# A cross-attention block on one NeuronCore: SBUF tiles at other addresses, softmax exponentials divided on GpSimd before they are turned, no turned inverses

## The chip, the cores and the metric

The kernel runs on one core of a Trainium2 chip. The metric is the device time of one execution in microseconds (us). Engines are named as the profile names them: PE (TensorE, with its weight loads as PEld), DVE (VectorE), ACT (ScalarE), POOL (GpSimd) and SP (SyncE, which here only issues DMAs). All arithmetic is fp32, with matrix products made of three fp32r products of high and low halves.

## The reference

128 sequences of 128 rows and 256 features go through one block: layer norm, self-attention of 16 heads of 16 features, a gated-in memory product, a second layer norm, and a feed-forward of 1024 hidden features. Cut to what matters:

```python
tgt1 = _layer_norm(tgt, g1, be1)
q = (x @ Wq.T + bq).reshape(b, s, H, HD)      # k and v alike
score = jnp.einsum('bshd,bthd->bhst', q, k) / math.sqrt(HD)
score = score + (1.0 - mask[:, None, :, :]) * -1000000000.0
p = jax.nn.softmax(score, axis=-1)
o = jnp.einsum('bhst,bthd->bshd', p, v).reshape(b, s, d)
tgt = tgt + (o @ Wo.T + bo)
tgt = tgt + (memory @ Wg.T + bg)
tgt1 = _layer_norm(tgt, g2, be2)
ff = jax.nn.relu(tgt1 @ W1.T + b1) @ W2.T + b2
return tgt + ff
```

The softmax needs, for each row of each head, the sum of 128 exponentials; the place where it is divided by that sum is free, since the division commutes with the product by v.

## The kernel before, in words

Two sequences make a group (GB = 2), so there are 64 groups. The program is written out as iterations i = -2 ... 65, and in iteration i five stages run side by side on different groups: `norm` (layer norm statistics of group i+2), `front` (turn, q, k and v of group i+1), `attn_` (scores and softmax of group i), `out_` (values, output projection, second layer norm of group i-1) and `ffn` (feed-forward of group i-2). Each iteration is cut into 13 ticks. Every engine has its own loop over the ticks, and tables such as `EXP_TICKS` and `TURN_TICKS` say at which tick it issues which piece. Nothing else sets the order: within an engine instructions run strictly in the order written, and across engines semaphores hold them.

A group has 8 chunks of 4 heads. A chunk k goes this way: PE writes its scores into one of two PSUM banks (`scores_of`), DVE adds the mask bias, takes the row minimum and writes to a ring of `scores` slots in SBUF ("mask k" below, L604), ACT takes exponentials in place with their row sums (`exponentials`, "exp k", L367, four instructions), PE turns the four 128x128 blocks into one of two `turn_ps` banks (`turn_chunk`, L850), and ACT copies them to `probs` (`copy_turned`, L377). The values product (`values_of`, L876) comes once all eight are copied.

The division before: DVE inverts the sums of four chunks at once (`invert_sums`, L547), POOL spreads them to 16 columns a head (`spread_inverses`, `inv_rows`, L704), PE turns those (`turn_inverses`, L860, four transposes), ACT copies the result to `inv` (L385), and DVE multiplies the finished values by `inv` while it takes them out of PSUM (`attn`, L624), then makes `attnT_hi` (L628) and `attnT_lo` (L567) from `attn`.

Other pieces that the prediction speaks of: `k_hi` on ACT (L436) and `k_lo`, `q_lo` on DVE (L651, L643), after which SP copies q and k into `q_stack` and `k_stack` by DMA for the next iteration's scores; `hT_hi` (DVE L634) and `hT_lo` (POOL L713), the halves of the hidden layer, four of each an iteration (numbered 0 to 3), that the down product waits for; `memT_hi` and `memT_lo` on POOL (L732, L713); `x_res` on POOL (L745), which `resid` on DVE (L577) waits for; then the second layer norm: `stats` (DVE L524), `var` and `rstd` (POOL L695, L697), `xhat2` (DVE L539, shown as xhat), and its turn on PE (L804), then the last quarter of the down product ("down3").

Of the kernel before, what the change touches and what calls it, by code (L numbers as in the profile page):

```python
# [45 lines left out]
INVERT_TICKS = (5, 9)  # L46
TURN_TICKS = (3, 4, 5, 7, 9, 10, 12)
# [21 lines left out]
def xattn_block(nc, x, memory, mask, wqT, wkT, wvT, woT, wgT, w1T, w2T,  # L69
# [13 lines left out]
    RING = 5  # L83
# [10 lines left out]
    with ExitStack() as ctx:  # L94
# [12 lines left out]
        vector_cols, at = {}, 0
        vec = sb("vec", [P, sum(n for _, n in VECTORS)])
        for name, n in VECTORS:
            vector_cols[name] = vec[:, at:at + n]  # L110
            at += n
        g1c, be1c, g2c, be2c, _, _, b1c = (vector_cols[name] for name, _ in VECTORS[:-1])
        qk_bias = sb("qk_bias", [P, 2 * KT])
        bqc, bkc = qk_bias[:, 0:KT], qk_bias[:, KT:2 * KT]
# [16 lines left out]
        stats1, mv1 = sb("stats1", [P, GB, 6]), sb("mv1", [P, GB, 2])  # L131
        var1, var2 = sb("var1", [P, GB]), sb("var2", [P, GB])
# [12 lines left out]
        row_min = sb("row_min", [P, CHUNKS, CH])  # L145
        row_sum, sum_inv = sb("row_sum", [P, CHUNKS, CH]), sb("sum_inv", [P, GB, KT, CPB, 2])

        inv_rows = sb("inv_rows", [P, GB, KT, P])
        be1w = inv_rows[:, 0]
        carrier = sb("carrier", [P, CHUNKS])  # L150
# [9 lines left out]
        stats2, mv2 = sb("stats2", [P, GB, 6]), sb("mv2", [P, GB, 2])  # L160
        rstd1, rstd2 = sb("rstd1", [P, GB]), sb("rstd2", [P, GB])
        one = sb("one", [P, H])
        eps, minus_half = sb("eps", [P, GB]), sb("minus_half", [P, GB])
        xhat2 = sb("xhat2", [P, GB, D])
        zT = [sb("zT_hi", [P, KT, ROWS], F32R), sb("zT_lo", [P, KT, ROWS], F32R)]
# [4 lines left out]
        y = sb("y", [P, GB, D])  # L170

# [33 lines left out]
        inv_spread = sem("inv_spread")  # L205
        inv_turned, inv_copied, attn_ready = sem("inv_turned"), sem("inv_copied"), sem("attn_ready")
# [51 lines left out]
        def loaded(name):  # L258
# [5 lines left out]
            if name in "qko":  # L264
                return {"q": attn, "k": inv, "o": resid}[name][:].rearrange("p k r -> p (k r)")
# [80 lines left out]
        def _(act):  # L346
# [33 lines left out]
            def copy_inverses(g):  # L380

                act.wait_ge(inv_turned, g + 1)
                if later(g):
                    act.wait_ge(attn_ready, g)
                act.activation(inv[:].rearrange("p k r -> p (k r)"), turn_ps[0][:, :], ACT.Copy  # L385
                               ).then_inc(inv_copied, 1)

            def iteration(i, norm, front, attn_, out_, ffn):
                for t in range(TICKS):
                    if out_ and t == 0:  # L390
                        copy_turned(i - 1, CHUNKS - 1)
                    if out_ and t == 1:
                        copy_inverses(i - 1)
# [8 lines left out]
                    if attn_ and t == 7:  # L402
                        copy_turned(i, TURN_TICKS.index(t))
# [9 lines left out]
                    if attn_ and t in TURN_TICKS and t != 7:  # L413
                        copy_turned(i, TURN_TICKS.index(t))
# [43 lines left out]
        def _(dve):  # L458
# [545 lines left out]
```

## Time and profile before

| | |
|---|---|
| median of 3 runs | 1834.77 us (1831.8 to 1836.27) |
| the profiled execution's own time | 1833.82 us |
| its span in the trace | 1832.2 us |
| PE busy, weight loads busy | 97%, 95% |
| ACT, DVE, POOL busy | 80%, 74%, 47% |
| SP's DMA queue (q1), share of 16 engines | 60.6% |
| granted TensorE clock, mean of the span | 0.989 |

Busy shares are of the span. The first 95 us and the last 35 us are ramps in which fewer than five stages run; between them each engine repeats one pattern of a little over 27 us, once for each group.

### The profile page before, as it was taken

To read this page: it belongs to the slowest core of one execution; us is meant where nothing else is said; L and a number is where in the kernel's file an instruction comes from. 1 tells how busy PE (TensorE), PEld (TensorE's weight loads), DVE (VectorE), ACT (ScalarE), POOL (GpSimd) and SP (SyncE) were. 2 spreads that over 40 slices of the span, in tenths; PEclk is the share of its full clock that TensorE was granted. 3 is DMA by queue.
4 is the path that set the end of the run, shared out by engine and by line. 5 is a ranking of instruction groups with operands and counts; after the bars stand their busy time and mean duration, and the time that the engine had idled before them with its cause. 6 is when DMAs were issued, how large, how long until landed. Compare 5 with 4: busy or idle time off the path is not lost.

```text
span 1832.2 us, 53739 instructions
## 1 busy us (share of the span) xinstructions
PE 1779.9 (97%) x17972; PEld 1746.4 (95%) x17972; DVE 1357.0 (74%) x6810; ACT 1464.7 (80%) x5577; POOL 867.6 (47%) x907
## 2 busy tenths in 40 slices
PE   5699999999999999999999999999999999999997
PEld 4699999999999999999999999999999999999997
DVE  5677777777777777777777777777777777777772
ACT  2788888887887888888887887888888887887882
POOL 2244544544544544544444444444454454454454
PEclk7799999999999999999999999999999999999999
DMA  6656656656656656656656656756756756756740
GB/s 157 84 87 112 98 98 110 98 98 110 99 98 109 99 98 110 100 98 109 100 98 108 104 96 106 107 93 107 110 92 105 109 93 105 112 91 103 110 71 18
DMA packets 148931, 183.66 MB, mean 100 GB/s; under 512 B 14768, under 2 KB 99120, under 8 KB 148656
## 3 DMA queue, kind: packets, MB, share of 16 engines
q1 hardware_dynamic: 148656, 180.23, 60.6%
q8 instruction: 144, 2.36, 0.6%
q14 instruction: 131, 1.07, 0.2%
HBM read 62.73 MB, written 16.78 MB: 43 GB/s over the span
## 4 chain that ended last, share of the span: by engine, by line
PE 95%; ACT 2%; issue 1%; DVE 0%; ACTq 0%
PE ffn_ps L787 13%; PE ffn_ps L789 13%; PE ffn_ps L788 13%; PE turn_ps L850 12%; PE work_ps L787 9%; PE work_ps L789 8%; PE work_ps L788 8%; PE score_ps L836 7%; PE value_ps L876 7%; PE work_ps L804 3%; PE turn_ps L860 2%; ACT scores L367 1%; ACT hid L410 0%; ACT probs L377 0%; DVE y L589 0%
## 5 line engine op out<-in xcount | busy, mean ns | idle before, releaser
L367 ACT ACTIVATE scores<-scores,row_min 128x128 f32<-128x128 f32 x2048 | 795.6, 400 | 8.9 <-DVE row_min L604 3.6
L713 POOL TENSOR_TENSOR hT_lo<-hid,hT_hi 128x512 fp32r<-128x512 f32 x256 | 355.4, 1388 | 587.5 <-DVE hT_hi L634 587.5
L377 ACT ACTIVATE probs<-turn_ps 128x512 f32<-128x512 f32 x512 | 303.0, 593 | 241.9 <-PE turn_ps L850 241.9
L604 DVE CUSTOM_DVE_ANT_0 scores<-score_ps,mask_bias 128x128 f32<-128x128 f32 x2048 | 470.8, 285 | 2.0 <-issue 2.0
L367 ACT ACTIVATION_READ_ACCUMULATOR scores<-scores,row_min 128x1 f32 x2048 | 407.0, 199 | 0.0
L850 PE MATMUL turn_ps<-ident,scores 128*128 128x128 f32 x2048 | 308.9, 274 | 4.5 <-ACT probs L377 4.5
L787 PE MATMUL ffn_ps<-zT_hi,w_lo 128*128 128x256 f32 x1024 | 304.2, 297 | 5.0 <-ACT hid L410 4.2
L787 PE MATMUL ffn_ps<-w_hi,hT_lo 128*128 128x256 f32 x1024 | 302.3, 295 | 2.4 <-ACT hid L410 2.4
L789 PE MATMUL ffn_ps<-zT_hi,w_hi 128*128 128x256 f32 x1024 | 289.5, 283 | 0.0
L788 PE MATMUL ffn_ps<-zT_lo,w_hi 128*128 128x256 f32 x1024 | 288.0, 281 | 0.0
L789 PE MATMUL ffn_ps<-w_hi,hT_hi 128*128 128x256 f32 x1024 | 286.6, 280 | 0.0
L788 PE MATMUL ffn_ps<-w_lo,hT_hi 128*128 128x256 f32 x1024 | 286.3, 280 | 0.0
L850 PEld LDWEIGHTS turn_ps<-ident,scores 128*128 128x128 f32 x2048 | 237.4, 141 | 5.7 <-ACT scores L367 5.5
L410 ACT ACTIVATE hid<-ffn_ps,vec 128x256 f32<-128x256 f32 x512 | 211.9, 467 | 22.4 <-PE ffn_ps L789 18.3
L836 PE MATMUL score_ps<-k_stack,q_stack 128*128 128x256 f32 x1024 | 200.3, 288 | 21.8 <-issue 12.9
L634 DVE CAST hT_hi<-hid 128x512 fp32r<-128x512 f32 x256 | 107.9, 421 | 146.1 <-ACT hid L410 146.1
L787 PEld LDWEIGHTS ffn_ps<-zT_hi,w_lo 128*128 128x128 f32 x1024 | 193.4, 189 | 6.7 <-ACT hid L410 5.2
L787 PEld LDWEIGHTS ffn_ps<-w_hi,hT_lo 128*128 128x128 f32 x1024 | 193.0, 188 | 3.0 <-ACT hid L410 3.0
L788 PEld LDWEIGHTS ffn_ps<-zT_lo,w_hi 128*128 128x128 f32 x1024 | 193.4, 189 | 0.0
L788 PEld LDWEIGHTS ffn_ps<-w_lo,hT_hi 128*128 128x128 f32 x1024 | 193.1, 189 | 0.0
L789 PEld LDWEIGHTS ffn_ps<-w_hi,hT_hi 128*128 128x128 f32 x1024 | 192.5, 188 | 0.0
L789 PEld LDWEIGHTS ffn_ps<-zT_hi,w_hi 128*128 128x128 f32 x1024 | 192.1, 188 | 0.0
(113 smaller groups left out, 4262.6 us busy)
## 6 DMA issues: line engine op xcount, KB each, us to landing
q_stack<-q_hi SPq DMA_DIRECT2D x128, 256.0 KB, 7.0
k_stack<-k_hi SPq DMA_DIRECT2D x256, 128.0 KB, 6.6
x_in<-x_dram SPq DMA_DIRECT2D x64, 256.0 KB, 3.4
mem_in<-memory_dram SPq DMA_DIRECT2D x64, 256.0 KB, 7.3
x_res<-x_dram SPq DMA_DIRECT2D x64, 256.0 KB, 7.5
q_stack<-q_lo SPq DMA_DIRECT2D x64, 256.0 KB, 4.2
k_stack<-k_lo SPq DMA_DIRECT2D x128, 128.0 KB, 6.6
out_dram<-y SPq DMA_DIRECT2D x64, 256.0 KB, 2.3
```

The lines of the kernel that those rows point to most:

```text
L367: last = act.activation(exps, exps, ACT.Exp, bias=row_min[:, k, h:h + 1], scale=-1.0, accum_out=row_sum[:, k, h:h + 1])
L377: act.activation(probs[:, k, :], turn_ps[k % 2][:, :], ACT.Copy).then_inc(probs_copied, 1)
L410: last = act.activation(hid[:, n % 2, j, :], ffn_ps[:, j * ROWS:(j + 1) * ROWS], ACT.Relu, bias=b1c[:, 2 * n + j:2 * n + j + 1])
L604: last = dve.tensor_tensor_reduce(out=scores[:, slot(i, t), h, :], in0=score_ps[t % 2][:, h * S:(h + 1) * S], in1=mask_bias[:, b, :], scal ...
L634: dve.tensor_copy(hT[0][:, 2 * n:2 * n + 2, :], hid[:, n % 2]).then_inc(hid_hi, 1)
L713: pool.tensor_tensor(halves[1], src, halves[0], ALU.subtract).then_inc(done, 1)
L787: pe.matmul(dst, lhs[1], rhs[0], start=start and j == 0, stop=False, **more)
L788: pe.matmul(dst, lhs[0], rhs[1], start=False, stop=False, **more)
L789: last = pe.matmul(dst, lhs[0], rhs[0], start=False, stop=stop and j == n - 1, **more)
L836: last = pe.matmul(score_ps[n % 2][:, k * 2 * S:(k + 1) * 2 * S], q_stack[i % 2][:, c, k, seq(b)], k_stack[i % 2][:, c, :, GB * k + b, :], ...
L850: last = pe.transpose(turn_ps[k % 2][:, h * S:(h + 1) * S], scores[:, slot(g, k), h, :], ident[:])
L876: last = pe.matmul(value_tiles[32 * c:32 * (c + 1), k, seq(b)], v_pad[g % 2][:, b, head_of(c, h), :], probs[:, CPB * b + c, h * S:(h + 1) ...
```

## The change

Three things are changed.

The division moves. DVE now inverts each chunk's four sums by themselves, right after that chunk's exponentials (eight reciprocals of 128x4 an iteration instead of two of 128x16). POOL then multiplies the chunk's 128x512 exponentials by them, in place in the ring (`divide`, eight instructions of 128x512 an iteration). PE waits for that (`exps_divided`) before it turns a chunk. `inv_rows`, `turn_inverses`, the copy to `inv` and the multiplication into `attn` are gone; `attnT_hi` and `attnT_lo` are made straight from PSUM, each a tick later.

The turns are one tick later (`TURN_TICKS`), the last chunk's turn and its copy move from tick 0 to tick 1 of the next iteration, the values product from tick 1 to 2; the ring has 7 slots instead of 5.

The SBUF tensors are declared in another order, with the small ones together. Before, the large tiles start at addresses that are 32, 64, 96 or other multiples of 32 past a multiple of 512 bytes: the weights 256, xT, q, k, the stacks and the ring 416, attnT and memT 320, zT, hid and hT 96. After, every large tile starts at a multiple of 512.

```diff
-INVERT_TICKS = (5, 9)
-TURN_TICKS = (3, 4, 5, 7, 9, 10, 12)
+INVERT_TICKS = (1, 2, 3, 4, 6, 7, 8, 10)
+DIVIDE_TICKS = (1, 2, 3, 4, 6, 7, 8, 10)
+TURN_TICKS = (4, 5, 6, 8, 9, 11, 12)
...
-    RING = 5
+    RING = 7
...
             def iteration(i, norm, front, attn_, out_, ffn):
                 for t in range(TICKS):
-                    if out_ and t == 0:
+                    if out_ and t == 1:
                         copy_turned(i - 1, CHUNKS - 1)
-                    if out_ and t == 1:
-                        copy_inverses(i - 1)
...
-            def invert_sums(i, b):
-                dve.wait_ge(exps_ready, CHUNKS * i + CPB * (b + 1))
+            def invert_sums(i, k):
+                dve.wait_ge(exps_ready, CHUNKS * i + k + 1)
                 if later(i):
-                    dve.wait_ge(inv_spread, GB * (i - 1) + b + 1)
-                dve.reciprocal(sum_inv[:, b], row_sum[:, CPB * b:CPB * (b + 1), :]
-                               .rearrange("p c (k e) -> p k c e", k=KT)).then_inc(sums_inverted, 1)
+                    dve.wait_ge(exps_divided, CHUNKS * (i - 1) + k + 1)
+                dve.reciprocal(sum_inv[:, k, :], row_sum[:, k, :]).then_inc(sums_inverted, 1)
...
-                    if out_ and t == 2:
+                    if out_ and t == 3:
                         g = i - 1
                         dve.wait_ge(attended, g + 1)
-                        dve.wait_ge(inv_copied, g + 1)
-                        if later(g):
-                            dve.wait_ge(attnT_split, g)
-                        dve.tensor_tensor(attn[:], value_tiles, inv[:], ALU.mult).then_inc(attn_ready, 1)
-                        dve.wait_ge(attn_ready, g + 1)
                         if later(g):
                             dve.wait_ge(proj_ready, g)
-                        dve.tensor_copy(attnT[0][:], attn[:]).then_inc(attnT_hi, 1)
+                        dve.tensor_copy(attnT[0][:], value_tiles).then_inc(attnT_hi, 1)
...
-                    if out_ and t == 3:
-                        split_low(attn[:], attnT, attnT_hi, i, attnT_split)
+                    if out_ and t == 4:
+                        split_low(value_tiles, attnT, attnT_hi, i, attnT_split)
...
-            def spread_inverses(g, b):
...
+            def divide(i, k):
+
+                pool.wait_ge(sums_inverted, CHUNKS * i + k + 1)
+                exps = scores[:, slot(i, k), :, :]
+                pool.tensor_tensor(exps, exps, sum_inv[:, k, :].unsqueeze(2).broadcast_to([P, CH, S]), ALU.mult
+                                   ).then_inc(exps_divided, 1)
...
-                    if attn_ and t == 6:
-                        spread_inverses(i, 0)
-                    if attn_ and t == 10:
-                        spread_inverses(i, 1)
+                    if attn_ and t in DIVIDE_TICKS:
+                        divide(i, DIVIDE_TICKS.index(t))
...
-                pe.wait_ge(exps_ready, CHUNKS * g + k + 1)
-                if k == 0 and later(g):
-                    pe.wait_ge(inv_copied, g)
+                pe.wait_ge(exps_divided, CHUNKS * g + k + 1)
...
-                    if out_ and t == 0:
+                    if out_ and t == 1:
                         turn_chunk(i - 1, CHUNKS - 1)
-                        turn_inverses(i - 1)
...
-                    if out_ and t == 1:
+                    if out_ and t == 2:
                         values_of(i - 1)
```

What stands in POOL's row, in a middle iteration, from tick 3 on. Before, from hT_lo 1 and 2 to the second spread; sums_inverted comes from DVE, ln2_mean from DVE's statistics of resid:

```order
L713 TENSOR_TENSOR hT_lo<-hid,hT_hi 128x512 [waits s_hid_hi] x2
L704 TENSOR_TENSOR inv_rows<-sum_inv,one 128x256 [waits inv_turned,sums_inverted]
L745 TENSOR_TENSOR x_res<-x_res,row 128x512 [waits xres_loaded]
L695 TENSOR_TENSOR var<-mv,eps 128x2 [waits ln2_ready,ln2_mean]
L697 TENSOR_TENSOR rstd<-var,minus_half 128x2 [waits ln2_var]
L713 TENSOR_TENSOR hT_lo<-hid,hT_hi 128x512 [waits s_hid_hi]
L695 TENSOR_TENSOR var<-mv,eps 128x2 [waits ln1_ready,ln1_mean]
L697 TENSOR_TENSOR rstd<-var,minus_half 128x2 [waits ln1_var]
L704 TENSOR_TENSOR inv_rows<-sum_inv,one 128x256 [waits inv_turned,sums_inverted]
```

The same stretch in the changed kernel, from divisions 2 and 3 to division 7:

```order
L682 TENSOR_TENSOR scores<-scores,sum_inv 128x512 [waits sums_inverted] x2
L688 TENSOR_TENSOR hT_lo<-hid,hT_hi 128x512 [waits s_hid_hi]
L682 TENSOR_TENSOR scores<-scores,sum_inv 128x512 [waits sums_inverted]
L718 TENSOR_TENSOR x_res<-x_res,row 128x512 [waits xres_loaded]
L682 TENSOR_TENSOR scores<-scores,sum_inv 128x512 [waits sums_inverted]
L674 TENSOR_TENSOR var<-mv,eps 128x2 [waits ln2_ready,ln2_mean]
L676 TENSOR_TENSOR rstd<-var,minus_half 128x2 [waits ln2_var]
L688 TENSOR_TENSOR hT_lo<-hid,hT_hi 128x512 [waits s_hid_hi]
L682 TENSOR_TENSOR scores<-scores,sum_inv 128x512 [waits sums_inverted]
L674 TENSOR_TENSOR var<-mv,eps 128x2 [waits ln1_ready,ln1_mean]
L676 TENSOR_TENSOR rstd<-var,minus_half 128x2 [waits ln1_var]
L682 TENSOR_TENSOR scores<-scores,sum_inv 128x512 [waits sums_inverted]
```

Division 4 now stands ahead of x_res, division 5 between x_res and the second layer norm's root, division 6 behind hT_lo 3; each waits for a reciprocal of DVE.

What stands in DVE's row around attnT_lo, before: tick 3, behind the second hT_hi and ahead of q_lo.

```order
L634 CAST hT_hi<-hid 128x512 [waits s_hid_relu]
L567 TENSOR_TENSOR attnT_lo<-attn,attnT_hi 128x512 [waits s_attnT_hi]
L643 SCALAR_TENSOR_TENSOR q_lo<-work_ps,qk_bias,q_hi 128x256 [waits q_high]
L643 SCALAR_TENSOR_TENSOR q_lo<-work_ps,qk_bias,q_hi 128x256
L601 MEMSET carrier 128x1 [waits scores_ready,probs_turned]
```

And in the changed kernel, from the second half of q_lo to attnT_lo in tick 4 (the rows between are mask 4, and the reciprocal is number 3):

```order
L622 SCALAR_TENSOR_TENSOR q_lo<-work_ps,qk_bias,q_hi 128x256
L585 MEMSET carrier 128x1 [waits scores_ready,probs_turned]
L588 ISA scores,row_min<-score_ps,mask_bias 128x128
L588 ISA row_min 128x1
L588 ISA scores,row_min<-score_ps,mask_bias 128x128
L588 ISA row_min 128x1
L588 ISA scores,row_min<-score_ps,mask_bias 128x128
L588 ISA row_min 128x1
L588 ISA scores,row_min<-score_ps,mask_bias 128x128
L588 ISA row_min 128x1
L532 RECIPROCAL sum_inv<-row_sum 128x4 [waits exps_divided,exps_ready]
L551 TENSOR_TENSOR attnT_lo<-value_ps,attnT_hi 128x512 [waits s_attnT_hi]
```

attnT_lo now stands behind mask 4 and behind a reciprocal that waits for the exponentials of chunk 3.

## Rows read from the trace of the kernel before

**Rows 1.** Busy time in the steady stretch: PE, PEld, DVE, ACT, POOL; then clock, DMA
```profile
400.00:800.00 400.00, 398.35 (x4082) 392.28 (x4075) 304.55 (x1546) 333.24 (x1278) 195.72 (x203) 1.00 0.63 101
```
**Rows 2.** Timeline of PE in one iteration: start us, length us, instructions, xcount
```profile
889.68 0.71 PE L836 MATMUL score_ps<-k_stack,q_stack 128*128 128x256 f32 x4 [0.44 <-issue]
...
890.67 0.60 PE L860 MATMUL turn_ps<-ident,inv_rows 128*128 128x128 f32 x4
891.10 0.60 PE L804 MATMUL work_ps<-ident,xhat 128*128 128x128 f32 x4
...
900.48 0.60 PE L850 MATMUL turn_ps<-ident,scores 128*128 128x128 f32 x4
...
902.95 0.36 PE L787 MATMUL work_ps<-wo_hi,attnT_lo 128*128 128x256 f32 x1
...
916.98 0.71 PE L836 MATMUL score_ps<-k_stack,q_stack 128*128 128x256 f32 x4
```
**Rows 3.** Timeline of PEld: weight loads of two products, first and last of each
```profile
903.62 0.19 PEld L787 LDWEIGHTS work_ps<-wg_hi,memT_lo 128*128 128x128 f32 x1
...
904.30 0.31 PEld L836 LDWEIGHTS score_ps<-k_stack,q_stack 128*128 128x128 f32 x2
...
909.92 0.19 PEld L787 LDWEIGHTS ffn_ps<-w_hi,hT_lo 128*128 128x128 f32 x1
...
911.20 0.19 PEld L789 LDWEIGHTS ffn_ps<-w_hi,hT_hi 128*128 128x128 f32 x1
```
**Rows 4.** DMA issues of the page: count, size, median us from issue to landing
```profile
k_stack<-k_hi SPq DMA_DIRECT2D x256, 128.0 KB, 6.6
```
**Rows 5.** Timeline of ACT around exp 3
```profile
900.68 0.84 ACT L436 ACTIVATE k_hi<-work_ps,qk_bias 128x256 fp32r<-128x256 f32 x2 [0.19 <-PE work_ps L789]
901.40 0.40 ACT L367 ACTIVATE scores<-scores,row_min 128x128 f32<-128x128 f32 x1
...
902.95 0.58 ACT L377 ACTIVATE probs<-turn_ps 128x512 f32<-128x512 f32 x1
```
**Rows 6.** Timeline of DVE, from mask 5 on
```profile
902.94 0.29 DVE L604 CUSTOM_DVE_ANT_0 scores<-score_ps,mask_bias 128x128 f32<-128x128 f32 x1
...
906.00 0.28 DVE L604 CUSTOM_DVE_ANT_0 scores<-score_ps,mask_bias 128x128 f32<-128x128 f32 x1
...
908.57 0.69 DVE L577 TENSOR_TENSOR resid<-work_ps,x_res 128x512 f32<-128x512 f32 x1 [1.65 <-issue]
...
910.34 0.29 DVE L604 CUSTOM_DVE_ANT_0 scores<-score_ps,mask_bias 128x128 f32<-128x128 f32 x1
...
911.47 0.73 DVE L539 TENSOR_SCALAR xhat<-resid,mv,rstd 128x256 f32<-128x256 f32 x2 [0.20 <-POOL rstd L697]
912.12 0.42 DVE L634 CAST hT_hi<-hid 128x512 fp32r<-128x512 f32 x1
912.99 0.25 DVE L547 RECIPROCAL sum_inv<-row_sum 128x16 f32<-128x16 f32 x1 [0.45 <-ACT scores L367]
```
**Rows 7.** Timeline of POOL
```profile
896.44 1.05 POOL L732 TENSOR_TENSOR memT_hi<-mem_in,one 128x512 fp32r<-128x512 f32 x1
...
905.37 1.29 POOL L713 TENSOR_TENSOR hT_lo<-hid,hT_hi 128x512 fp32r<-128x512 f32 x1 [3.16 <-DVE hT_hi L634]
...
907.19 1.29 POOL L745 TENSOR_TENSOR x_res<-x_res,row 128x512 f32<-128x512 f32 x1
910.46 0.19 POOL L695 TENSOR_TENSOR var<-mv,eps 128x2 f32<-128x2 f32 x1 [1.98 <-DVE mv L531]
```
**Rows 8.** Timeline of DVE, attnT_hi
```profile
896.54 1.23 DVE L628 CAST attnT_hi<-attn 128x512 fp32r<-128x512 f32 x1
```
**Rows 9.** Busy times by stretch, columns as in rows 1
```profile
57.60:61.00 3.40, 1.63 (x13) 1.18 (x11) 0.51 (x6) 3.40 (x16) 0.00 (x0) 1.00 1.03 140
...
88.30:95.00 6.70, 3.21 (x15) 3.24 (x16) 3.05 (x13) 0.84 (x2) 1.00 (x1) 0.50 0.86 168
...
1797.00:1822.00 25.00, 19.23 (x149) 17.81 (x148) 7.88 (x16) 5.68 (x14) 13.29 (x12) 1.00 0.04 12
```

More of the change, by code:

```diff
@@ L102, in sem @@
             return ctx.enter_context(nc.semaphore(name))
+        row_min = sb("row_min", [P, CHUNKS, CH])
+        row_sum, sum_inv = sb("row_sum", [P, CHUNKS, CH]), sb("sum_inv", [P, CHUNKS, CH])
         ident = sb("ident", [P, P])
[L107 to L114, printed above, removed]
         row = sb("row", [P, 4, D])
@@ L144, in xattn_block @@
         scores = sb("scores", [P, RING, CH, S])
[L145 to L150, printed above, removed]
         probs = sb("probs", [P, CHUNKS, CH * S])
-        inv = sb("inv", [P, KT, ROWS])
-        attn = sb("attn", [P, KT, ROWS])
+        early = sb("early", [P, KT * D])
         attnT = [sb("attnT_hi", [P, KT, ROWS], F32R), sb("attnT_lo", [P, KT, ROWS], F32R)]
@@ L159, in xattn_block @@
         resid = sb("resid", [P, GB, D])
[L160 to L163, printed above, removed]
         xhat2 = sb("xhat2", [P, GB, D])
+        be1w = xhat2[:, 0, :].rearrange("p (k s) -> p k s", k=KT)
         zT = [sb("zT_hi", [P, KT, ROWS], F32R), sb("zT_lo", [P, KT, ROWS], F32R)]
@@ L170, in xattn_block @@
         y = sb("y", [P, GB, D])
+        vector_cols, at = {}, 0
+        vec = sb("vec", [P, sum(n for _, n in VECTORS)])
+        for name, n in VECTORS:
+            vector_cols[name] = vec[:, at:at + n]
+            at += n
+        g1c, be1c, g2c, be2c, _, _, b1c = (vector_cols[name] for name, _ in VECTORS[:-1])
+        qk_bias = sb("qk_bias", [P, 2 * KT])
+        bqc, bkc = qk_bias[:, 0:KT], qk_bias[:, KT:2 * KT]
+        stats1, mv1 = sb("stats1", [P, GB, 6]), sb("mv1", [P, GB, 2])
+        var1, var2 = sb("var1", [P, GB]), sb("var2", [P, GB])
+        carrier = sb("carrier", [P, CHUNKS])
+        stats2, mv2 = sb("stats2", [P, GB, 6]), sb("mv2", [P, GB, 2])
+        rstd1, rstd2 = sb("rstd1", [P, GB]), sb("rstd2", [P, GB])
+        one = sb("one", [P, H])
+        eps, minus_half = sb("eps", [P, GB]), sb("minus_half", [P, GB])
         score_ps = [bank("score_ps0"), bank("score_ps1")]
@@ L264, in loaded @@
             if name in "qko":
-                return {"q": attn, "k": inv, "o": resid}[name][:].rearrange("p k r -> p (k r)")
+                return early[:] if name == "k" else {"q": resid_b2, "o": resid}[name][:].rearrange("p b n -> p (b n)")
             at, n = {"v": (0, 1), "1": (1, 4)}[name]
@@ L852, in turn_chunk @@
                 last.then_inc(probs_turned, 1)
-            def turn_inverses(g):
-                pe.wait_ge(inv_spread, GB * (g + 1))
-                pe.wait_ge(probs_copied, CHUNKS * g + CHUNKS - 1)
-                for k in range(KT):
-                    for b in range(GB):
-                        last = pe.transpose(turn_ps[0][:, k * ROWS + b * S:k * ROWS + (b + 1) * S],
-                                            inv_rows[:, b, k, :], ident[:])
-                last.then_inc(inv_turned, 1)
             def values_of(g):
```

25 lines of the change are left out of this document (3 added, 22 removed).

## The prediction

> **What bounds the kernel now.** I read the busy shares by stretch first. Between the ramps PE is busy 398.4 of 400 us, ACT 333, DVE 305, POOL 196 [rows 1]: PE has no room, the others do. Then PE's timeline: an iteration is 27.30 us from score product to score product, with a wait of 0.44 us ahead of the first one [rows 2]. The trace names no releaser for that wait. The product also waits for k_stack, whose six copies SP issues one after the other behind k_lo and which land 6.6 us after their issue [rows 4], so I put it down to them: PE's work sets the period, and the k_stack copies come a few tenths late in some iterations. Last I read ACT, DVE and POOL around the places that the change touches, since a division put between exponential and turn makes POOL part of every chunk's path.
>
> **What PE is spared.** turn_inverses takes 891.10 - 890.67 = 0.43 us an iteration [rows 2], 64 times 27 us. The copy to inv (ACT) and the product attn (DVE) go too, but these engines wait for PE now, so they give nothing by themselves.
>
> **Addresses.** Six steps of the product of memT by wg take 904.30 - 903.62 = 0.68 us, 0.113 a step; eleven of hT by w2 take 1.28, 0.116 [rows 3]. The first pair lies at 320 and 256 past multiples of 512, the second at 96 and 256: where one operand starts at an odd multiple of 32 bytes the step is longer by 0.003 to 0.006. With all at 512 I take 0.113 for all. Some 150 of 172 such steps an iteration would gain 0.004: 0.6 us, 0.3 of it ahead of the k projection's end. Bounds: nothing, and 1.0 us if steps fall below 0.113. "SBUF — State Buffer", section "Door 1: The DMA port swizzle", of the Trainium skill says that reads cost by lines of 16 bytes; all operands start at multiples of 32 already, so by that rule the addresses change no step and the period below would be 30.7 instead of 30.4. Rows 3 speak mildly against the rule.
>
> **The division's own price.** POOL has no row of this form. memT_hi, 128x512 with one operand spread over the columns, takes 1.05 us; x_res, with two full operands, 1.29 [rows 7]. The division spreads one operand, so I take 1.05 and keep 1.29 as the upper bound. Eight of them are 8.4 us; POOL goes from 13.4 us an iteration (196 of 400 [rows 1]) less the two spreads to about 20.6 of 27. By busy time it fits. The order is what matters, since POOL and DVE run strictly in the order written.
>
> **One iteration, step by step, in us after its first score product** (step lengths are differences of starts in the rows):
> First, the k projection ends at 10.80 (900.48 - 889.68 [rows 2]) before; without the inverses and with chunk 0's turn now behind it, 0.43 each, and 0.3 for addresses, at 9.65. Up to here PE is the limit.
> Second, k_hi and exp 3 follow on ACT, 902.95 - 900.48 = 2.47 [rows 5], and the last sum 0.1 later: 12.2. DVE inverts (0.25 for 16 columns [rows 6], I take 0.2): 12.4. Now attnT_lo stands behind this reciprocal. Nearest row is resid, which reads PSUM at the same size: 0.69 [rows 6]. It is ready at 13.1. PE reaches the output projection after chunk 0's turn, an up product, a score product and chunk 1's turn, which took 902.95 - 900.48 = 2.47 before too [rows 2]: at 12.0. **Wait A: 1.1 us.**
> Third, DVE goes on with mask 5, statistics, hT_hi and k_lo, 906.00 - 902.94 = 3.06 [rows 6] less the reciprocal of 0.16 that is no longer there: 16.0. Mask 6 and reciprocal 4 (mask 7 took 0.93 to its end: 911.47 - 910.34 less 0.20 idle; then 0.2): 17.1. For DVE's delay by POOL (below) 0.3: 17.4.
> Fourth, POOL has division 4 ahead of x_res: 18.4. x_res to resid is 908.57 - 907.19 = 1.38: 19.8. resid to mask 7 is 1.77: 21.6. Mask 7 and reciprocal 5, 1.1: 22.7. POOL's root of the second layer norm needed only the statistics before and ran beside mask 7; now it stands behind division 5, which waits for reciprocal 5: division 5 ends at 23.7, root (911.47 - 910.46 = 1.01 [rows 6, 7]) at 24.8, xhat2 and hT_hi 3 (0.65 and 0.42 [rows 6]) at 25.9, hT_lo 3 (1.29 [rows 7]) at 27.15, division 6 at 28.2.
> Fifth, PE may now turn chunk 6, then xhat2 (0.43 each) and make down3 (12 steps, 1.37): 30.4. The next iteration starts.
> PE itself would be ready sooner. From the projection to the next iteration it took 916.98 - 902.95 = 14.03 [rows 2]; one chunk's turn more, turn 6 and what follows (2.23) and 0.5 for addresses and the wait at the end less, 11.7: 24.8 from 13.1. It waits some 0.7 ahead of turn 5 (23.0 against 23.7) and then **wait B: 2.5 us** ahead of turn 6.
>
> **Sum.** 30.4 against 27.30, and against a mean a little above that (the wait for k_stack differs between iterations): +3.0 us. All five stages run in 62 iterations: +186 us on the profiled execution's 1833.8, which is 0.9 below the median: 2020. The chain is one loop through all engines, so what is off PE's path otherwise, such as ACT (83% busy), hides nothing of it.
>
> **DVE and POOL in each other's way.** attnT_hi as a cast within SBUF took 1.23 us [rows 8] where the cast hT_hi of the same size takes 0.42 [rows 6]: it began 0.10 after memT_hi on POOL and ended 0.28 after it [rows 7, 8]. POOL is now busy with division 1 and memT when the second hT_hi comes; that cast waits for memT_lo, q_lo and mask 4 come late, and with them reciprocal 3: the 0.3 above (between 0 and 1.0). "SBUF — State Buffer", section "Who interferes with whom", of the Trainium skill says that such a cast and a GpSimd instruction exclude each other for their whole length; the trace agrees with its 1.23 us. By the rule alone every one of four casts could wait up to a division, and the period would reach 32.5 instead of 30.4, as two casts stand on the loop (2 times 1.05). POOL stands idle when both come, so I don't take it.
>
> **The clock.** With PE waiting, its clock can fall. In the first ramp it was 2.4 GHz (1.00) over a stretch in which PE was busy 1.63 of 3.40 us, and 1.2 GHz after such waits; one stretch at 1.2 GHz lasted 6.7 us [rows 9]. In the last ramp, with 19.23 of 25 us busy and every wait 0.9 us, it stayed at 2.4 [rows 9]. Wait B, 2.5 us, lies on the side of the first. It is followed by the serial part of the loop, so 6.7 us at half speed cost 3.3 us of period. If it falls in one iteration out of three: 1.1 us, +70 us.
>
> **The rivals.**
> A (0.42), the forecast: the loop above, and the clock falls behind wait B in some iterations. 2090; 2040 to 2230, the last if it falls in each.
> B (0.25): the loop, clock stays. 2020; 1985 with the least address, cast and lock prices, 2065 with divisions of 1.29 us (three on the loop, +0.7).
> C (0.13): a step of the loop is shorter than I have it, so that only wait A is left. The loop through POOL gives PE nothing to wait for if division 6 ends by 24.9, 3.3 us sooner. Then 27.3 - 0.43 - 0.6 - 0.3 + 1.1 = 27.1 if the gain of the addresses is whole, 27.7 if none: 1820 to 1860, and up to 1985 for what lies between.
> D (0.15), faster: PE stays the limit through all, as its busy share says. The mechanism would be that ACT reaches exp 3 and exp 4 sooner than now because copies are fewer, and DVE reciprocals 3 and 4 with it, early enough that x_res starts at 14 instead of 18.4; from there the price turns. Then 27.4 - 0.43 - 0.6 - 0.4 = 26.0: 1745. Against it: k_hi, which exp 3 stands behind, waits for PE, not for ACT (0.19 us idle [rows 5]).
> E (0.05): gains of 0.43 and 0.6 and wait A cancel within 0.3% (what a measurement of this kernel can just tell): 1835. That the k_stack copies hold the period whatever PE does belongs here: 27.3 stays unless q and k are ready sooner.
>
> **How the numbers follow.** The loop (A and B) is 0.67. The range takes in both, and of C the upper half down to 1890: about 0.8 lies within 1890 to 2200; the top is cut at 2200, since a clock that falls every time needs waits that fall at the same place each time. A and B alone: 1985 to 2200. Slower: A, B, and most of C, 0.79; same 0.05; faster 0.16, D and a bit of C.
>
> **What the profile after would show.** Right: PE's longest waits are turn_ps for scores divided by POOL, twice an iteration, and work_ps for attnT_lo; period 30 to 33; PE busy under 90%; DVE resid right behind x_res; POOL under 80% busy though it sets the pace; a division at 1.05; steps at 0.113; clock below 0.97. Wrong: turn waits under 0.5 us, or POOL idle ahead of x_res with DVE's reciprocal long done. The prediction fails if mask 6 and reciprocal 4 come much before 17 us, or if POOL's division takes under 0.7 us.

## The result, and the profile after

The changed kernel takes 2058.69 us, the median of 4 runs (2058.62 to 2061.07), against 1834.51 for the kernel before in the same comparison (4 runs, 1831.8 to 1836.27). The ratio is 1.123, with a 95% interval of 1.122 to 1.124: slower by 12%. The profiled execution took 2058.62 us, with a span of 2057.0 and a mean granted TensorE clock of 0.981. The forecast was 2090 with a range of 1890 to 2200.

The busy times in the same stretch as in [rows 1] (PE, PEld, DVE, ACT, POOL, then clock and DMA share):

```profile
400.00:800.00 400.00, 362.84 (x3569) 348.92 (x3570) 268.80 (x1436) 289.80 (x1114) 255.38 (x258) 0.99 0.54 90
```

PE was busy 398 of 400 us, now 363. Every other engine is idle for longer too, except POOL, whose work per iteration grew. No engine is full, so something makes them wait in turn. The groups of the page say who waits for whom (count, then busy us and mean ns, then idle us before and its releaser):

```profile
L682 POOL TENSOR_TENSOR scores<-scores,sum_inv 128x512 f32<-128x512 f32 x512 | 528.2, 1042 | 253.2 <-DVE sum_inv L532 253.2
...
L821 PEld LDWEIGHTS turn_ps<-ident,scores 128*128 128x128 f32 x2048 | 235.2, 141 | 153.7 <-POOL scores L682 152.7
...
L613 DVE CAST hT_hi<-hid 128x512 fp32r<-128x512 f32 x256 | 172.3, 673 | 47.3 <-ACT hid L395 47.3
...
k_stack<-k_hi SPq DMA_DIRECT2D x256, 128.0 KB, 5.7
```

PE waits 153 us for divisions, POOL waits 253 us for reciprocals. A division takes 1.042 us. The casts hT_hi take 0.67 in the mean, so some are much longer than the 0.42 of [rows 6]. The k_stack copies land after 5.7 us, not 6.6 [rows 4], and no longer matter: in the steady iterations the last of them lands 3.9 us or more before the score product wants it.

One middle iteration of PE, which stands against [rows 2]. The first score product begins at 806.90; the next iteration's at 837.70:

```profile
806.90 0.64 PE L809 MATMUL score_ps<-k_stack,q_stack 128*128 128x256 f32 x4
807.62 0.63 PE L777 MATMUL work_ps<-ident,xhat 128*128 128x128 f32 x4
...
820.69 0.39 PE L760 MATMUL work_ps<-wo_hi,attnT_lo 128*128 128x256 f32 x1 [0.70 <-DVE attnT_lo L551]
...
835.33 0.66 PE L821 MATMUL turn_ps<-ident,scores 128*128 128x128 f32 x4 [2.09 <-POOL scores L682]
...
837.70 0.64 PE L809 MATMUL score_ps<-k_stack,q_stack 128*128 128x256 f32 x4
```

The period is 30.80 us, with a wait of 0.70 ahead of the output projection and one of 2.09 ahead of the turn of chunk 6 (0.94 and 2.29 for the weight loads that go before them).

The same iteration on ACT and on DVE. Exponential 3 stands behind k_hi, reciprocal 3 behind it, attnT_lo behind that; later resid, xhat2 and, in the last row, the front's xhat:

```profile
817.48 0.84 ACT L421 ACTIVATE k_hi<-work_ps,qk_bias 128x256 fp32r<-128x256 f32 x2 [1.14 <-PE work_ps L762]
818.21 0.40 ACT L364 ACTIVATE scores<-scores,row_min 128x128 f32<-128x128 f32 x1
```

```profile
816.37 1.51 DVE L613 CAST hT_hi<-hid 128x512 fp32r<-128x512 f32 x1
817.80 0.87 DVE L622 SCALAR_TENSOR_TENSOR q_lo<-work_ps,qk_bias,q_hi 128x256 fp32r<-128x256 f32 x2
...
819.88 0.18 DVE L532 RECIPROCAL sum_inv<-row_sum 128x4 f32<-128x4 f32 x1 [0.37 <-ACT scores L364]
819.97 0.66 DVE L551 TENSOR_TENSOR attnT_lo<-value_ps,attnT_hi 128x512 fp32r<-128x512 f32 x1
...
824.36 0.17 DVE L532 RECIPROCAL sum_inv<-row_sum 128x4 f32<-128x4 f32 x1
826.97 0.69 DVE L561 TENSOR_TENSOR resid<-work_ps,x_res 128x512 f32<-128x512 f32 x1 [2.45 <-issue]
...
831.86 0.73 DVE L524 TENSOR_SCALAR xhat<-resid,mv,rstd 128x256 f32<-128x256 f32 x2 [2.03 <-POOL rstd L676]
...
836.23 1.44 DVE L524 TENSOR_SCALAR xhat<-x_in,mv,rstd 128x256 f32<-128x256 f32 x2 [2.25 <-POOL rstd L676]
```

And POOL in the same iteration, from memT_lo to division 7 (the last row):

```profile
816.30 1.29 POOL L688 TENSOR_TENSOR memT_lo<-mem_in,memT_hi 128x512 fp32r<-128x512 f32 x1
...
824.61 1.04 POOL L682 TENSOR_TENSOR scores<-scores,sum_inv 128x512 f32<-128x512 f32 x1 [0.42 <-DVE sum_inv L532]
825.61 1.28 POOL L718 TENSOR_TENSOR x_res<-x_res,row 128x512 f32<-128x512 f32 x1
829.84 1.04 POOL L682 TENSOR_TENSOR scores<-scores,sum_inv 128x512 f32<-128x512 f32 x1 [2.96 <-DVE sum_inv L532]
830.84 0.20 POOL L674 TENSOR_TENSOR var<-mv,eps 128x2 f32<-128x2 f32 x1
831.12 0.70 POOL L676 TENSOR_TENSOR rstd<-var,minus_half 128x2 f32<-128x2 f32 x1
833.01 1.27 POOL L688 TENSOR_TENSOR hT_lo<-hid,hT_hi 128x512 fp32r<-128x512 f32 x1 [1.19 <-DVE hT_hi L613]
834.23 1.04 POOL L682 TENSOR_TENSOR scores<-scores,sum_inv 128x512 f32<-128x512 f32 x1
...
836.16 1.04 POOL L682 TENSOR_TENSOR scores<-scores,sum_inv 128x512 f32<-128x512 f32 x1
```

Read crosswise: reciprocal 4 ends, division 4 begins at once; x_res follows it, resid follows x_res (its wait is named "issue", but it begins 0.08 after x_res ends); mask 7 and reciprocal 5 follow resid, division 5 follows with 2.96 us of idle POOL before it; the root follows division 5, xhat2 the root; then hT_lo 3, division 6, and PE's turn of chunk 6 begins 0.06 after it. These steps follow one another without overlap, each on its own engine, while PE works on other chunks beside them and then waits for the end of the chain.

### The profile page after: what moved, and what is told of

Same layout as the page of the kernel before. It is cut to its first block and busy times, and to the rows that moved or that the text cites. A ratio compares the mean times of both kernels' runs of the same rounds, so it can differ in the third digit from the quotient of the medians.

```text
span 2057.0 us, 53926 instructions
## 1 busy us (share of the span) xinstructions
PE 1826.7 (89%) x17716; PEld 1751.3 (85%) x17716; DVE 1353.7 (66%) x7130; ACT 1441.8 (70%) x5513; POOL 1277.7 (62%) x1291
## 3 DMA queue, kind: packets, MB, share of 16 engines
q14 instruction: 137, 1.12, 0.2%
## 5 line engine op out<-in xcount | busy, mean ns | idle before, releaser
L364 ACT ACTIVATE scores<-scores,row_min 128x128 f32<-128x128 f32 x2048 | 796.1, 397 | 20.1 <-DVE row_min L588 15.4
L682 POOL TENSOR_TENSOR scores<-scores,sum_inv 128x512 f32<-128x512 f32 x512 | 528.2, 1042 | 253.2 <-DVE sum_inv L532 253.2
L688 POOL TENSOR_TENSOR hT_lo<-hid,hT_hi 128x512 fp32r<-128x512 f32 x256 | 330.2, 1290 | 360.8 <-DVE hT_hi L613 360.8
L760 PE MATMUL ffn_ps<-w_hi,hT_lo 128*128 128x256 f32 x1024 | 309.8, 303 | 1.9 <-ACT hid L395 1.9
L762 PE MATMUL ffn_ps<-w_hi,hT_hi 128*128 128x256 f32 x1024 | 293.9, 287 | 0.0
L761 PE MATMUL ffn_ps<-w_lo,hT_hi 128*128 128x256 f32 x1024 | 293.7, 287 | 0.0
L809 PE MATMUL score_ps<-k_stack,q_stack 128*128 128x256 f32 x1024 | 212.1, 300 | 14.6 <-DMA k_stack<-k_hi 6.9
L613 DVE CAST hT_hi<-hid 128x512 fp32r<-128x512 f32 x256 | 172.3, 673 | 47.3 <-ACT hid L395 47.3
L760 PEld LDWEIGHTS ffn_ps<-w_hi,hT_lo 128*128 128x128 f32 x1024 | 200.5, 196 | 2.6 <-ACT hid L395 2.6
L761 PEld LDWEIGHTS ffn_ps<-w_lo,hT_hi 128*128 128x128 f32 x1024 | 200.6, 196 | 0.0
L762 PEld LDWEIGHTS ffn_ps<-w_hi,hT_hi 128*128 128x128 f32 x1024 | 200.0, 195 | 0.0
```

The lines of the kernel that those rows point to most:

```text
L364: last = act.activation(exps, exps, ACT.Exp, bias=row_min[:, k, h:h + 1], scale=-1.0, accum_out=row_sum[:, k, h:h + 1])
L613: dve.tensor_copy(hT[0][:, 2 * n:2 * n + 2, :], hid[:, n % 2]).then_inc(hid_hi, 1)
L682: pool.tensor_tensor(exps, exps, sum_inv[:, k, :].unsqueeze(2).broadcast_to([P, CH, S]), ALU.mult).then_inc(exps_divided, 1)
L688: pool.tensor_tensor(halves[1], src, halves[0], ALU.subtract).then_inc(done, 1)
L760: pe.matmul(dst, lhs[1], rhs[0], start=start and j == 0, stop=False, **more)
L761: pe.matmul(dst, lhs[0], rhs[1], start=False, stop=False, **more)
```

## The experiments

All are compared with the kernel before on the same chip. In the expectations "the kernel after" is the changed kernel.

**The addresses alone.** The kernel before, with its SBUF tiles declared so that the large ones start at multiples of 512:

```diff
+        row_min = sb("row_min", [P, CHUNKS, CH])
+        row_sum, sum_inv = sb("row_sum", [P, CHUNKS, CH]), sb("sum_inv", [P, GB, KT, CPB, 2])
...
-        stats1, mv1 = sb("stats1", [P, GB, 6]), sb("mv1", [P, GB, 2])
-        var1, var2 = sb("var1", [P, GB]), sb("var2", [P, GB])
...
-        row_min = sb("row_min", [P, CHUNKS, CH])
-        row_sum, sum_inv = sb("row_sum", [P, CHUNKS, CH]), sb("sum_inv", [P, GB, KT, CPB, 2])
...
+        stats1, mv1 = sb("stats1", [P, GB, 6]), sb("mv1", [P, GB, 2])
+        var1, var2 = sb("var1", [P, GB]), sb("var2", [P, GB])
```

> The kernel before with only the SBUF tiles declared in another order, so that every large tile starts at a multiple of 512 bytes; nothing else is changed. Theory 1, from the changed kernel's trace, where the weight loads of all 256-column products follow each other by 0.120 us instead of 0.113 to 0.118: these addresses make PE's steps longer. 172 steps by 0.0025 to 0.003 are 0.45 us an iteration, and PE is the limit here, so about +28 us: 1863 (1850 to 1875). Theory 2, that of the prediction: steps at 0.113, about -38 us: 1797. Theory 3: k_stack's copies land sooner (5.7 us after issue instead of 6.6) and that alone counts, -0.2 us an iteration: 1822.

1836.35 us, ratio 1.0014 (1.0004 to 1.0023): no gain, and none of the three times expected. Two steps of the product of memT by wg, weight loads:

```profile
903.43 0.19 PEld L786 LDWEIGHTS work_ps<-wg_hi,memT_lo 128*128 128x128 f32 x1
903.55 0.19 PEld L787 LDWEIGHTS work_ps<-wg_lo,memT_hi 128*128 128x128 f32 x1
```

0.120 a step where [rows 3] have 0.113. Most iterations are 27.46 us long (mean 27.48) and PE waits 0.2 us at most, while the kernel before varies between 27.21 and 27.94 (mean 27.43), with waits ahead of the first score product of up to 0.65. In its trace 42 of 60 steady iterations load the weights of this product 0.06 us after the last k_stack copy has landed, so these waits are for k_stack, as the prediction took them; here it is 13 of 60. So the addresses do two things of opposite sign: PE's steps get longer, by 0.25 us an iteration, and the k_stack copies come 0.2 us sooner (6.4 us in the median).

**The division without the addresses.** The changed kernel with the old order of declarations:

> The changed kernel with the tiles at the addresses that they had before (the ring with its 7 slots, all others in the old order); all instructions and waits as in the changed kernel. Theory 1: the loop holds, and some 58 steps of PE ahead of the k projection's end and 12 in the last down product are 0.0025 us shorter: -0.2 us an iteration, about 2046 (2040 to 2055). Rival, that the addresses have to do with the slowdown itself, by slower accesses of DVE and POOL: well under 1950.

2052.32 us, ratio 1.1188 (1.1169 to 1.1206), period mostly 30.7. Of the 224 us lost, the addresses are worth 6 to 8 (the first by the times, the second by the ratios); the rest belongs to the division and the order around it.

**x_res out of the chain.** In the changed kernel the whole block of x_res moves from tick 6 to tick 0, behind division 7 of the group before:

```diff
+                    if out_ and t == 0:
...
+                        pool.wait_ge(xres_loaded, 16 * i)
...
-                    if out_ and t == 6:
...
-                        pool.wait_ge(xres_loaded, 16 * i)
```

> The changed kernel with one move: POOL adds the bias to x_res at tick 0, behind the last division of the group before, instead of at tick 6 behind division 4. Theory, the loop of the prediction: resid no longer waits for division 4 and x_res. In the trace of the changed kernel resid starts 20.07 us after the iteration's start; without them it could start at 17.6. Wait B (2.1 us ahead of turn 6) is then gone and the period falls from 30.8 to 28.7, where PE is the limit with wait A; the clock no longer falls. About 1920 (1900 to 1935). Rival: another link, such as the k_stack copies or the exponentials, sets the pace at nearly the same time: above 2020.

1947.16 us, ratio 1.0615 (1.0598 to 1.0633): half of the loss is gone, and so is the wait for division 6. The period is mostly 29.3, more than the expected 1920 us asks for. POOL and DVE at the seam of two iterations:

```profile
795.29 1.04 POOL L682 TENSOR_TENSOR scores<-scores,sum_inv 128x512 f32<-128x512 f32 x1
796.29 1.34 POOL L705 TENSOR_TENSOR x_res<-x_res,row 128x512 f32<-128x512 f32 x1
```

```profile
795.37 2.41 DVE L524 TENSOR_SCALAR xhat<-x_in,mv,rstd 128x256 f32<-128x256 f32 x2 [1.72 <-POOL rstd L676]
797.71 0.68 DVE L551 TENSOR_TENSOR zT_lo<-work_ps,zT_hi 128x512 fp32r<-128x512 f32 x1
```

```profile
798.50 0.42 PEld L777 LDWEIGHTS work_ps<-ident,xhat 128*128 128x128 f32 x4 [1.12 <-DVE xhat L524]
```

The two xhat instructions of the front begin with division 7 and end 0.15 us after x_res, 2.41 us where the undisturbed pair takes 0.73. The turn of xhat waits for it and for zT_lo behind it, 1.1 us. x_res was moved into a place where it holds DVE up. Six steady iterations of the same run show what this costs. In them x_res comes later, as here, where it waits for its own load:

```profile
531.90 1.04 POOL L682 TENSOR_TENSOR scores<-scores,sum_inv 128x512 f32<-128x512 f32 x1
533.66 1.28 POOL L705 TENSOR_TENSOR x_res<-x_res,row 128x512 f32<-128x512 f32 x1 [0.72 <-DMA x_res<-x_dram]
```

```profile
531.97 1.44 DVE L524 TENSOR_SCALAR xhat<-x_in,mv,rstd 128x256 f32<-128x256 f32 x2 [1.72 <-POOL rstd L676]
```

The pair takes 1.44 us, held by division 7 alone, the turn of xhat waits less than 0.2, and the iteration that begins there is 28.4 us long instead of 29.3. So the hold by x_res costs 1.0 us of period.

**The root ahead of division 5.** Only the second layer norm's root moves, by one place in POOL's order:

```diff
+                    if out_ and t == 7:
+                        inverse_root(i - 1, mv2, var2, rstd2, ln2_mean, ln2_var, ln2_ready, ln2_rstd)
                     if attn_ and t in DIVIDE_TICKS:
                         divide(i, DIVIDE_TICKS.index(t))
-                    if out_ and t == 7:
-                        inverse_root(i - 1, mv2, var2, rstd2, ln2_mean, ln2_var, ln2_ready, ln2_rstd)
```

> The changed kernel with one move: at tick 7 POOL computes the root of the second layer norm ahead of division 5 instead of behind it. Theory, the loop of the prediction: the root runs beside mask 7 as it did before, xhat2 starts at about 23.0 instead of 24.96 after the iteration's start, hT_lo 3 is held by division 5 until 24.1, division 6 ends 1.9 us sooner: period about 28.9, about 1930 (1910 to 1950). Rival, that POOL's sheer number of instructions is what costs: nothing is taken away here, so over 2040.

1970.53 us, ratio 1.0744 (1.0726 to 1.0761), period 29.6. The wait for division 6 falls from 2.09 to 0.89 us. The period fell by 1.2 us, and 1.9 was expected: xhat2 now runs beside division 5 (POOL from 827.94) and takes 0.74 us longer than its 0.73:

```profile
827.98 1.47 DVE L524 TENSOR_SCALAR xhat<-resid,mv,rstd 128x256 f32<-128x256 f32 x2
```

**attnT_lo a tick sooner**, ahead of reciprocal 3:

```diff
-                    if out_ and t == 4:
+                    if out_ and t == 3:
                         split_low(value_tiles, attnT, attnT_hi, i, attnT_split)
```

> The changed kernel with one move: DVE makes attnT_lo at tick 3, behind attnT_hi, instead of at tick 4 behind mask 4 and reciprocal 3. Theory, the loop of the prediction: wait A (0.94 us of the weight loads ahead of the output projection) is gone, and mask 5 with all that follows comes 0.6 us sooner, so the period falls from 30.8 to 30.2 and no further, since wait B is set by what stands behind on POOL: 2020 (2005 to 2035). Rival: wait B takes up all that wait A gave, since it hangs on reciprocal 3 and exp 3 alone: 2055 to 2060.

One run: 2037.57 us, just above the range expected. An ordinary iteration is 30.36 us instead of 30.80, so taking wait A (0.94) away is worth 0.44; the wait for division 6 grows from 2.09 to 2.30. The clock fell more often, 17 times instead of 12 (mean 0.977), which ate a part of the gain. Why it did is open.

**Other addresses for the kernel before**: one small tile of 64 bytes ahead of the rings and activations, so that they start 64 past multiples of 512 and the weights at multiples of 512:

```diff
+        shift64 = sb("shift64", [P, 16])
         x_in = sb("x_in", [P, GB, D])
```

> The kernel before with the weights at multiples of 512 bytes and all other large tiles 64 bytes past such multiples. Theory 1: the steps of 0.113 us that memT by wg showed in the kernel before come from the two operands lying 64 bytes apart (256 and 320). Then most 256-column steps are 0.113 here too, against 0.120 with both at 512: PE needs about 0.8 us an iteration less than in the kernel before, but k_stack's copies then set the period, which falls little: 1815 to 1830. Theory 2: the 0.113 is of that product alone, for another reason: steps stay at 0.117 to 0.120, 1830 to 1840.

1840.52 us, ratio 1.0033 (1.0024 to 1.0043), above what either theory had. PE's steps are shorter than at 512 (0.113 to 0.118), its shortest iteration 26.96 us, but the k_stack copies land after 6.9 us and PE waits up to 1.0 us for them; in 58 of 60 iterations the score product starts 0.06 us behind their landing. The mean period is 27.5. Here the copies, not PE, set the pace, so shorter steps gain nothing. Why the copies take longer is open.

**All four pieces moved.** attnT_lo at tick 3, the second root ahead of division 5, the front's root at tick 6 instead of 8, and x_res at tick 0 but behind resid_b, away from xhat:

```diff
-                    if out_ and t == 4:
+                    if out_ and t == 3:
                         split_low(value_tiles, attnT, attnT_hi, i, attnT_split)
...
+                    if out_ and t == 7:
+                        inverse_root(i - 1, mv2, var2, rstd2, ln2_mean, ln2_var, ln2_ready, ln2_rstd)
                     if attn_ and t in DIVIDE_TICKS:
                         divide(i, DIVIDE_TICKS.index(t))
-                    if out_ and t == 7:
-                        inverse_root(i - 1, mv2, var2, rstd2, ln2_mean, ln2_var, ln2_ready, ln2_rstd)
-                    if norm and t == 8:
+                    if norm and t == 6:
                         inverse_root(i + 2, mv1, var1, rstd1, ln1_mean, ln1_var, ln1_ready, ln1_rstd)
-                    if out_ and t == 6:
-                        pool.wait_ge(xres_loaded, 16 * i)
...
                                            ALU.add).then_inc(resid_biased, 1)
+                    if out_ and t == 0:
+                        pool.wait_ge(xres_loaded, 16 * i)
```

> The changed kernel with four moves and nothing taken away: attnT_lo at tick 3 (as alone in another run), x_res at tick 0 behind resid_b, the root of the first layer norm at tick 6 behind division 4, the root of the second ahead of division 5. Theory: every wait of PE longer than a few tenths is gone, and PE is the limit: 27.46 (the kernel before at these addresses) less 0.44 for the inverses, 27.0 us an iteration, 1805 (1795 to 1830). So the change's own saving shows only when POOL's order is mended. Rival: with eight divisions more, POOL and DVE collide so often on SBUF that a loop over 28 us stays: over 1860.

1822.01 us, ratio 0.9927 (0.991 to 0.9943): faster than both kernels, with the same eight divisions. Its busy times, and a stretch of POOL's timeline:

```profile
400.00:800.00 400.00, 399.96 (x4075) 392.68 (x4074) 310.45 (x1633) 325.78 (x1268) 293.84 (x297) 1.00 0.62 102
```

```profile
818.76 1.04 POOL L682 TENSOR_TENSOR scores<-scores,sum_inv 128x512 f32<-128x512 f32 x1 [0.44 <-DVE sum_inv L532]
819.76 0.20 POOL L674 TENSOR_TENSOR var<-mv,eps 128x2 f32<-128x2 f32 x1
820.04 0.70 POOL L676 TENSOR_TENSOR rstd<-var,minus_half 128x2 f32<-128x2 f32 x1
820.70 0.20 POOL L674 TENSOR_TENSOR var<-mv,eps 128x2 f32<-128x2 f32 x1
820.98 0.69 POOL L676 TENSOR_TENSOR rstd<-var,minus_half 128x2 f32<-128x2 f32 x1
821.63 1.04 POOL L682 TENSOR_TENSOR scores<-scores,sum_inv 128x512 f32<-128x512 f32 x1
```

PE is full again, POOL is busy 73% of the stretch. After division 4 stand the two roots and division 5 without a gap, where the changed kernel had x_res and 2.96 us of idleness. Nearly every iteration is 27.20 us. The turns a tick later and the ring of 7 slots are still there, so they are not what cost the changed kernel its time. Of the 0.43 us that turning the inverses took, 0.26 shows against the kernel before at the same addresses (27.46); where the rest goes is open. The front's root was not moved by itself, so its share is not known.

**Half of the division.** The changed kernel dividing only the first 64 of each head's 128 columns; the other half stays undivided, so this kernel leaves half of that work out:

```diff
-                exps = scores[:, slot(i, k), :, :]
-                pool.tensor_tensor(exps, exps, sum_inv[:, k, :].unsqueeze(2).broadcast_to([P, CH, S]), ALU.mult
+                exps = scores[:, slot(i, k), :, 0:S // 2]
+                pool.tensor_tensor(exps, exps, sum_inv[:, k, :].unsqueeze(2).broadcast_to([P, CH, S // 2]), ALU.mult
```

> The changed kernel in which POOL divides only the first 64 of each head's 128 columns, so that the other half stays undivided; every instruction and wait is still there. Theory: three divisions stand on the loop (4, 5 and 6). By memT_hi (512 columns, 1.05 us) and the spreads (256 columns, 0.62 us) each gets 0.43 us shorter, so the period falls by 1.3 us to 29.5 and the clock stays up: about 1975 (1955 to 1990). Rival, all eight in a row count: -3.4 us an iteration, 1850. Rival, POOL's price does not count, only the order: over 2040.

One run: 1945.32 us, below the 1955 to 1990 expected. A division of 128x256 takes 0.614 us instead of 1.042, and the period is 29.26 instead of 30.80:

```profile
L682 POOL TENSOR_TENSOR scores<-scores,sum_inv 128x256 f32<-128x256 f32 x512 | 311.8, 614 | 328.1 <-DVE sum_inv L532 328.1
```

0.43 us less a division moved the period by 1.54, more than the three divisions on the chain (4, 5 and 6) account for (1.28). The rest, 0.26, is where the front's xhat pair stands beside division 7: its first instruction takes 0.69 us here and 1.12 in the changed kernel (0.41 undisturbed), PE's turn of xhat begins 0.24 us sooner after the first score product and the k projection ends 0.28 sooner.

**The moved pieces with the old addresses**, the edits of the two runs above that moved the four pieces and restored the old order of declarations:

> The changed kernel with the four pieces moved as in e7_all_moved, and the tiles at the addresses of the kernel before. With tiles at 512 multiples this order gave 1822.0 and a constant period of 27.20 us in which PE waited for nothing. Theory 1: PE's steps fall back to 0.113 to 0.118 here and nothing else is on the path, so the period falls by what the addresses cost the kernel before, 0.25 us an iteration: 26.95, 1806 (1800 to 1812). Theory 2: the k_stack copies land later again (6.6 instead of about 5.7 us after their issue), and since they ended only 0.1 to 0.8 us before PE wanted them, they set the period in most iterations: 27.1 to 27.5, 1815 to 1840, no faster than with the new addresses. I hold theory 2 the likelier, 1825.

1816.78 us, ratio 0.9914 (0.9896 to 0.9931). Theory 1's 1806 is out. The interval overlaps that of the new addresses, so a difference between the two is not shown. PE's shortest iteration is 26.83 us, but k_stack lands after 6.9 us (49 of 60 score products start 0.06 us behind it, 6 of 60 with the new addresses) and the periods vary from 26.83 to 27.82, mean 27.15 against 27.21. Again most of what the shorter steps give comes back as waits.

## Why the prediction was right, step by step

**The loop through all engines: right.** With stations counted from the first score product, the chain was predicted and measured so:

| | predicted | measured |
|---|---|---|
| k projection ends | 9.65 | 10.4 |
| attnT_lo ready | 13.1 | 13.7 |
| reciprocal 4 ends | 17.4 | 17.6 |
| resid begins | 19.8 | 20.1 |
| division 5 begins | 22.7 | 22.9 |
| xhat2 begins | 24.8 | 25.0 |
| division 6 ends | 28.2 | 28.4 |
| next iteration | 30.4 | 30.8 |

Two terms inside the chain were wrong and cancelled. The k projection ended 0.7 late (see the addresses below). From there to the end of reciprocal 4 the chain took 7.25 us instead of the 7.75 predicted: the 0.3 for DVE's delay by POOL was not paid there (last paragraph of this section), and the rest are tenths. That the later stations agree within 0.3 is in part luck.

**Wait A, predicted 1.1 us, is 0.94; wait B, predicted 2.5, is 2.29** (weight loads). The small wait of 0.7 ahead of turn 5 did not come: PE was later by as much as its k projection. The moves confirm both causes: taking x_res out of the chain removes wait B, taking the root from behind division 5 more than halves it, and an earlier attnT_lo removes wait A. And the division itself, at 1.04 us (1.05 was taken), is no cost by its amount: with all eight of them in a better order the kernel is faster than before. What it cost was its place: x_res and the root stood behind divisions that waited for DVE, and attnT_lo behind reciprocal 3.

**Addresses: the wrong sign.** The term "With all at 512 I take 0.113 for all", a gain of 0.6 us an iteration, failed. The steps became 0.118 to 0.120. The two products of [rows 3] were no fair sample either: in the kernel before the product of xT by wv, with operands at 416 and 256, already took 0.121 a step, 1.33 us for eleven.

```profile
908.03 0.19 PEld L787 LDWEIGHTS work_ps<-wv_hi,xT_lo 128*128 128x128 f32 x1
...
909.36 0.19 PEld L789 LDWEIGHTS work_ps<-wv_hi,xT_hi 128*128 128x128 f32 x1
```

Measured alone, PE loses 0.25 us an iteration (27.46 against the 27.21 of the iterations with the least wait) and the earlier k_stack copies return it. In the changed kernel the k projection ends at 10.4 instead of 9.65, and the 0.3 us that was taken off for addresses is the largest part of that; the old addresses would bring it only 0.04 sooner. Another part is the front's xhat, held by division 7 for 1.44 us; zT_lo behind it and then PE's turn at 807.62 come 0.24 later than in the kernel with all four moved. The remaining 0.15 or so is not explained. The Trainium skill, "SBUF — State Buffer", section "Door 1: The DMA port swizzle", prices reads by lines of 16 bytes, and by that the addresses change nothing; the product of memT by wg, 0.113 a step before and 0.120 when only the order of declarations is changed, shows that here they do, though by 6% at most.

**The clock: right in kind, far too large.** The forecast had a fall in one iteration of three, each 6.7 us long and worth 3.3 us, 70 us in all. It fell twelve times, for 3.4 us each time, which cost 1.2 us: both the number and the length were too high. Ten of the falls came in five pairs of neighbouring iterations. The first fall of one pair (columns as above):

```profile
987.80:990.10 2.30, 0.80 (x7) 0.80 (x8) 0.16 (x1) 0.10 (x1) 2.22 (x4) 1.00 0.24 69
990.10:990.90 0.80, 0.80 (x8) 0.80 (x7) 0.69 (x1) 0.80 (x2) 0.80 (x2) 0.88 0.00 0
990.90:994.10 3.20, 3.20 (x17) 3.20 (x16) 2.80 (x12) 0.18 (x1) 0.90 (x2) 0.50 0.26 82
994.10:1000.00 5.90, 5.90 (x66) 5.77 (x69) 3.85 (x30) 5.68 (x23) 2.88 (x3) 1.00 0.13 44
```

It goes to 1.2 GHz 1.4 us after PE resumes from wait B and stays there for 3.4 us; by the weight loads of the first score product, the iteration from 960.75 is 31.44 long, the next 32.77, and the one after 30.53: 2.3 us over three times 30.80. Summed over all iterations the excess over 30.80 is 14 us. The same wait stands in all the other iterations, without a fall; why it comes in those is open.

**The sum.** The steady iteration was 0.4 longer than predicted (25 us in 62 of them) and the clock 56 us cheaper: 2090 + 25 - 56 = 2059. Two errors of opposite sign brought the forecast close, which is luck; the period, 30.4 against 30.8, is what was really foretold. The loss itself is 3.37 us (30.80 less 27.43) times 62, 209 us, and the clock's 14.

**DVE held by POOL: a right effect at the wrong place.** The prediction had the second hT_hi held by memT_lo and the delay, 0.3 us, arrive at reciprocal 3. hT_hi was held: it took 1.51 us beside memT_lo and ended 0.3 after it. But mask 4 was done at 819.51, and DVE then waited 0.37 us for exponential 3, so the hold cost the chain nothing. With half the division the same cast took 0.66 us, and reciprocal 3 began 2.61 us after the end of the k projection in both kernels. Where the hold did cost was a place that the prediction had no term for, the front's xhat ahead of the next k projection: 1.44 us beside division 7. The Trainium skill, "SBUF — State Buffer", section "Who interferes with whom", has such instructions exclude each other; the 2.41 us of xhat across two POOL instructions agree. The bound of 32.5 by the rule alone did not come: of the four casts hT_hi of an iteration only one was held, the others took 0.39 to 0.43 us. In the kernels with moved pieces the hold took 1.0 us of the gain (x_res at tick 0) and, as far as xhat2's 0.74 us tells, most of what was missing with the root ahead.

**The signs named ahead.** The period, resid right behind x_res, POOL under 80% busy (64% of the stretch) and the division's 1.04 us came as named, and PE's busy share just so (91% of the stretch, 89% of the span, where under 90 was named). Three did not: the steps were not 0.113; the clock was 0.981, not below 0.97; and the turns of divided scores were waited for once an iteration, not twice.

## What to carry to other kernels

Cost a new step by what stands behind it in the strict order of its engine, not by its length: eight divisions of 1.04 us cost 224 us with x_res and a root behind waiting divisions, and nothing with the four pieces moved. Before moving a POOL instruction into an idle place, see whether DVE then casts or normalizes within SBUF: here it was held until the POOL instruction had ended, and whether that cost anything hung on what DVE would have waited for next. And where PE and a DMA finish within a few tenths of each other, a shorter PE step is given back as a wait.

## What the hardware showed that was not expected

A matmul step of 128x256 with the weight load of 128x128 took 0.118 to 0.120 us with both operands at multiples of 512 bytes. At other addresses it took 0.113 to 0.121: 0.113 for memT and wg at 320 and 256, 0.117 for hT and w2 at 96 and 256, 0.121 for xT and wv at 416 and 256, 0.113 to 0.118 with the activations 64 past a multiple and the weights at one. Round addresses were faster by 0.001 us at most and slower by up to 0.007; which offsets are fast was not found.

The k_stack copies of 128 KB took 6.6 to 6.9 us in kernels with the old or 64-shifted addresses and full PE, 6.4 or 6.5 with 512 multiples, and 4.8 to 5.9 us in most of the kernels in which PE waits. What sets their time was not tested.

GpSimd's product with one operand spread over the columns took 1.042 us for 512 elements and 0.614 for 256: if the time is linear in the elements, about 0.19 us is fixed (an estimate from two sizes).

The clock fell in pairs of neighbouring iterations, the pairs 280 to 370 us apart, though each iteration had the same waits, the longest mostly 2.1 us. With attnT_lo a tick sooner and a longest wait of 2.3 us it fell every third to fifth iteration and never in two in a row. In the kernels whose longest wait was 1.3 us or less (the root ahead, x_res early, half the division) it did not fall once between the ramps.
